# A Mixture-of-Experts, SSM, Mixture-of-Experts block: the middle stage rebuilt, its statistics moved into the expert phase, and TensorE summing the two rotated-back parts

## The reference

```python
x = x + 0.5 * ffn(layernorm(x))     # 8 experts, each token uses the one with the largest logit
x = x + ssm(layernorm(x))           # a diagonal complex recurrence over the 4096 tokens
x = x + 0.5 * ffn(layernorm(x))     # the same weights again

# ffn: logits = x @ Wr; e = argmax; out = softmax(logits)[e] * (gelu(x @ W1[e] + b1[e]) @ W2[e] + b2[e])
# ssm: h_t = a * h_(t-1) + B' @ u_t   (128 complex states);   y_t = real(C @ h_t)
```

## Time and profile before

| | |
|---|---|
| median of 3 runs | 738.88 us (729.33, 738.88, 741.73) |
| the profiled execution | 745.37 us, of which the span from first to last instruction is 743.5 us |
| mean granted PE clock | 0.869 of 2.4 GHz |
| busy share PE, DVE, ACT, POOL | 79%, 71%, 53%, 44% |
| expert phases | 104 to 343 us and 486 to 743 us |
| middle | 343 to 464 us |
| routing | 464 to 486 us |

### The profile page before, as it was taken

How to read it: one execution, slowest core, us unless ns; L and a number is a source line. 1 busy time by engine, 2 the same in 40 slices (tenths; PEclk the granted TensorE clock), 3 DMA queues, 4 the chain that set the end, 5 groups by cost and what they waited for, 6 DMA issues and landing times.

```text
span 743.5 us, 18466 instructions
## 1 busy us (share of the span) xinstructions
PE 589.5 (79%) x6396; PEld 518.0 (70%) x6396; DVE 531.1 (71%) x1204; ACT 396.8 (53%) x879; POOL 330.0 (44%) x310
## 2 busy tenths in 40 slices
PE   5960149999999899994477878139999999999997
PEld 5950138998888787893245657129998778988886
DVE  5869967778886775784499993927776666766675
ACT  4877846565554555552336653107555546546463
POOL 0031183555545453531477881162555454554532
PEclk9555559999999999998658895558999999999999
DMA  8993031111111111113102211030111111111210
GB/s 276 374 375 122 5 99 31 40 45 43 49 45 38 35 51 37 38 30 99 51 29 90 80 57 57 1 103 19 44 51 44 36 50 36 45 41 36 50 36 2
DMA packets 34872, 51.86 MB, mean 70 GB/s; under 512 B 6747, under 2 KB 27933, under 8 KB 34528
## 3 DMA queue, kind: packets, MB, share of 16 engines
q1 hardware_dynamic: 24800, 31.90, 12.6%
q0 software_dynamic: 9984, 18.79, 9.0%
...
...
## 4 chain that ended last, share of the span: by engine, by line
PE 68%; DVE 18%; issue 7%; DMA 3%; ACT 2%; POOL 1%; SPq 1%; ACTq 0%; POOLq 0%; DVEq 0%
PE bank L1065 31%; PE bank L1082 9%; PE bank L1083 9%; PE bank L1084 9%; PE bank L982 4%; PE bank L1041 3%; DVE stats L580 3%; DVE weights_arena L613 2%; PE bank L976 2%; DMA weights_arena<-L_attn_u 2%; DVE weights_arena L920 1%; DVE weights_arena L757 1%; DVE weights_arena L917 1%; DVE weights_arena L942 1%; DVE ev L927 1%
## 5 line engine op out<-in xcount | busy, mean ns | idle before, releaser
L519 ACT ACTIVATE weights_arena<-bank,b1t,inv 128x128 f32<-128x128 f32 x624 | 228.4, 467 | 211.2 <-PE bank L1065 161.2
L1065 PE MATMUL bank<-weights_arena 128*128 128x128 f16 x3744 | 239.2, 222 | 23.5 <-issue 17.5
L1065 PEld LDWEIGHTS bank<-weights_arena 128*128 x3744 | 220.6, 99 | 39.8 <-issue 37.0
L1082 PE MATMUL bank<-weights_arena 128*128 x624 | 170.2, 273 | 1.2 <-issue 1.0
L1083 PE MATMUL bank<-weights_arena 128*128 x624 | 170.1, 273 | 1.3 <-issue 1.1
L1084 PE MATMUL bank<-weights_arena 128*128 x624 | 170.1, 273 | 0.9 <-issue 0.6
L816 DVE TENSOR_SCALAR weights_arena<-weights_arena,hscale 128x512 f16<-128x512 f32 x156 | 76.8, 492 | 83.6 <-ACT weights_arena L519 77.4
L819 DVE SCALAR_TENSOR_TENSOR weights_arena<-weights_arena,hscale 128x512 f16<-128x512 f32 x156 | 117.3, 752 | 5.6
L375 POOL DMA_INDIRECT recf<-records,sorti x78 | 81.4, 1043 | 23.8 <-issue 23.8
L381 POOL DMA_INDIRECT out<-weights_arena,sorti x39 | 39.5, 1013 | 112.7 <-DVE weights_arena L835 99.8
L381 POOL DMA_INDIRECT x_after_ffn<-weights_arena,sorti x39 | 40.6, 1040 | 105.3 <-DVE weights_arena L835 95.8
...
## 6 DMA issues: line engine op xcount, KB each, us to landing
...
recf<-records,sorti POOLq DMA_INDIRECT x78
weights_arena<-L_attn_u,sorti POOLq DMA_INDIRECT x39
x_after_ffn<-weights_arena,sorti POOLq DMA_INDIRECT x39
```

Of the source, the lines that this page charges most:

```text
L519: last = act.activation(hb[q % 2][:, f, :], src, ACT.Gelu, bias=b1t[:, bass.ds(e * FC + f, 1)], scale=inv1[:, bass.ds(e, 1)])
L1065: last = pe.matmul(acc[:, f * P:(f + 1) * P], weights[wpart * DC + d], xts[q % 2][:, xpart, d, :], start=(n == 0), stop=(n == 5))
L1082: pe.matmul(acc, hs[q % 2][:, 0, f, :], high, start=(f == 0), stop=False)
```

## The change

- In the first expert phase DVE takes mean and variance of each finished tile, and POOL its inverse root, deviation and shift. They travel with the rows, in four more columns (rows of 260 numbers instead of 256). The middle loop no longer has `row_stats` for its input.
- The router's logits for the second feed-forward are made by linearity: PE multiplies the transposed normalised input of the recurrence by the centred Wr (`route_logits` right after the B product), DVE scales it back by the deviation (`lt`), and the y product has nine more columns (C times centred Wr, and the row mean), so that DVE only adds. The second normalising, transposing and logit product of the finished rows is gone. ACT takes the variance by squaring finished rows with a running sum, and one inverse root over all tokens follows on POOL after the loop.
- POOL no longer adds the two rotated-back parts: the y product takes both parts, one after the other, into the same PSUM columns (two products for each 128 tokens instead of one). POOL's list now has the sine product of chunk c+1 ahead of the two rotations back of chunk c.
- `zz` has three buffers, `mod` and `uts` two. The state's turn is two small DVE instructions instead of four.
- In both routings one `tensor_scalar` over 1280 numbers becomes a `tensor_tensor`, and 32 small `tensor_scalar` become 4 `tensor_tensor`.

```diff
-LATE = 4
 XS = 5
+XW = D + 4
+MEAN, RSTD, STD, SHIFT = range(D, XW)
+YW = D + E + 1
...
+        zz = [view(11856 + k * 2 * CH, 2, CH) for k in range(3)]
+        waste = view(14928, 3, D, dt=BF16)
+        angle = view(12288, 2, CH)
...
+        psum = ctx.enter_context(nc.psum_tensor("banks", [P, 8, 512], F32))
+        bank = [psum[:, k, :] for k in range(8)]
+        ys = psum[:, 4:8, :]
...
                     pool.wait_ge(s["o"], q + 1)
+                    o = og[q % 2] if ph == 1 else og[q % 2][:, 0:D]
+                    if ph == 1:
+                        ve = ve1[:, q % 2:q % 2 + 1]
+                        pool.wait_ge(o_ve, q + 1)
+                        chain.link(pool.tensor_tensor(o[:, RSTD:RSTD + 1], ve, mhalf[:, 0:1], ALU.pow))
+                        pool.tensor_tensor(o[:, STD:STD + 1], ve, o[:, RSTD:RSTD + 1], ALU.mult)
+                        chain.link(pool.tensor_scalar(o[:, SHIFT:SHIFT + 1], o[:, MEAN:MEAN + 1], -1.0,
+                                                      o[:, RSTD:RSTD + 1], ALU.mult, ALU.mult))
                     pool.indirect_dma_start(dst, bass.IndirectOffsetOnAxis(ap=sorti[:, q, 2:3].bitcast(U32), axis=0),
-                                            og[q % 2], None, bounds_check=T - 1, oob_is_err=False) \
+                                            o, None, bounds_check=T - 1, oob_is_err=False) \
                         .then_inc(s["scat"][q % RING], 16)
...
-            for c in range(-2, NC + 1):
...
+            def rotated(n):
+                pool.wait_ge(s_gs, n + 1)
+                if n >= 2:
+                    pool.wait_ge(s_zi, n - 1)
+                pool.tensor_tensor(mod[n % 2][:, 1, :], gs, turn[:, 1, :], ALU.mult).then_inc(s_mi, 1)
+            rotated(0)
+            for c in range(NC):
+                z = zz[c % 3]
+                if c + 1 < NC:
+                    rotated(c + 1)
+                pool.wait_ge(s_sp, c + 1)
+                pool.tensor_tensor(z[:, 0, :], z[:, 0, :], back[:, 0, :], ALU.mult).then_inc(s_b0, 1)
+                pool.tensor_tensor(z[:, 1, :], z[:, 1, :], back[:, 1, :], ALU.mult).then_inc(s_aa, 1)
+            pool.wait_ge(s_sq, NJ)
+            chain.link(pool.tensor_scalar(ve2[:], ssq[:], 1.0 / D, EPS, ALU.mult, ALU.add))
+            chain.link(pool.tensor_tensor(rstd, ve2[:], mhalf[:], ALU.pow))
+            pool.tensor_tensor(shift, nm2[:], rstd, ALU.mult).then_inc(s_rstd, 1)
             ffn(2, x2_dram, out)
...
             for c in range(-2, NC + 2):
-                if 0 <= c + 1 < NC:
-                    act.wait_ge(s_ut, c + 2)
-                    if c >= 0:
-                        act.wait_ge(s_g, c + 1)
+                n = c + 1
+                if 0 <= n < NC:
+                    act.wait_ge(s_ut, n + 1)
+                    if n >= 2:
+                        act.wait_ge(s_a, n - 1)
                     for d in range(DC):
-                        last = act.copy(uts[:, d, :], bank[d][:])
+                        last = act.copy(uts[n % 2][:, d, :], bank[d])
                     last.then_inc(s_uts, 1)
-                if c >= 2:
...
+                n = c + 2
+                if n < NC:
+                    act.wait_ge(sx[n % XS], 16 * (n // XS) + 16)
                     if n >= 2:
                         act.wait_ge(s_ut, n - 1)
-                    normalise(xs[n % XS], uns[n % 2], lambda i: nb[:, n % 2, i:i + 1],
-                              lambda i: rs[:, n % 2, i:i + 1], s_nb, n + 1, s_un)
+                    x = xs[n % XS]
+                    for i in range(CT):
+                        last = act.activation(uns[n % 2][:, i, :], x[:, i, 0:D], ACT.Identity, bias=x[:, i, SHIFT:SHIFT + 1],
+                                              scale=x[:, i, RSTD:RSTD + 1])
+                    last.then_inc(s_un, 1)
+                n = c + 1
+                if 0 <= n < NC:
+                    act.wait_ge(s_g, n + 1)
+                    if n >= 1:
+                        act.wait_ge(s_mi, n)
+                        act.wait_ge(s_in, n)
+                    act.copy(gs, bank[2]).then_inc(s_gs, 1)
+                b = c - 2
+                if 0 <= b < NC:
+                    act.wait_ge(s_x2, b + 1)
+                    act.wait_ge(s_m2, b + 1)
+                    for i in range(CT):
+                        j = b * CT + i
+                        if j >= 3:
+                            act.wait_ge(s_sq, j - 2)
+                        act.activation(waste[:, j % 3, :], xs[b % XS][:, i, 0:D], ACT.Square, bias=nm2[:, j:j + 1],
+                                       accum_out=ssq[:, j:j + 1]).then_inc(s_sq, 1)
...
-                dve.tensor_scalar(sval[:, :, 1, :], q1, part[:], None, ALU.mult).then_inc(s["pos"], 1)
+                dve.tensor_tensor(sval[:, :, 1, :], q1, part_b[:].unsqueeze(2).to_broadcast([P, NJ, NTE]), ALU.mult).then_inc(s["pos"], 1)
             def route_rows(ph, g):
-                for j in range(GR * g, GR * g + GR):
-                    last = dve.tensor_scalar(onerow[:, j, :], iota_b[:], slot_f[:, j:j + 1], None, ALU.is_equal)
-                last.then_inc(S[ph]["row"], 1)
+                slot_b = placed[ph][10]
+                rows = slice(GR * g, GR * g + GR)
+                dve.tensor_tensor(onerow[:, rows, :], iota_b[:].unsqueeze(1).to_broadcast([P, GR, P]),
+                                  slot_b[:, rows].unsqueeze(2).to_broadcast([P, GR, P]),
+                                  ALU.is_equal).then_inc(S[ph]["row"], 1)
...
+                        dve.wait_ge(s["o"], q + 1)
+                        dve.bn_stats(st1[:], o[:, 0:D]).then_inc(o_stat, 1)
+                        dve.wait_ge(o_stat, q + 1)
+                        dve.bn_aggr(o[:, MEAN:MEAN + 2], st1[:]).then_inc(o_mean, 1)
+                        dve.wait_ge(o_mean, q + 1)
+                        dve.tensor_scalar(ve1[:, q % 2:q % 2 + 1], o[:, MEAN + 1:MEAN + 2], EPS, None, ALU.add) \
+                            .then_inc(o_ve, 1)
...
-            for c in range(-2, NC + LATE):
...
+            for c in range(NC + 1):
+                if c < NC:
+                    m, z = mod[c % 2], zz[c % 3]
                     dve.wait_ge(s_gs, c + 1)
-
-                    dve.tensor_tensor(mod[:, 0, :], gs, turn[:, 0, :], ALU.mult).then_inc(s_in, 1)
+                    dve.tensor_tensor(m[:, 0, :], gs, turn[:, 0, :], ALU.mult).then_inc(s_in, 1)
                     dve.wait_ge(s_in, c + 1)
-                    if c >= 1:
-                        dve.wait_ge(s_aa, c)
-                    dve.tensor_tensor_scan(zz[:, 0, :], rho[:].to_broadcast([P, CH]), mod[:, 0, :], state[:, 0:1],
+                    if c >= 3:
+                        dve.wait_ge(s_y, c - 2)
+                    dve.tensor_tensor_scan(z[:, 0, :], rho[:].to_broadcast([P, CH]), m[:, 0, :], state[:, 0:1],
                                            ALU.mult, ALU.add).then_inc(s_zr, 1)
+                    dve.wait_ge(s_a, c + 1)
+                    dve.tensor_tensor(lt[:, c % 2], bank[3][:, 0:CT * E].rearrange("p (i e) -> p i e", e=E),
+                                      xs[c % XS][:, :, STD:STD + 1].to_broadcast([P, CT, E]), ALU.mult).then_inc(s_lt, 1)
                     dve.wait_ge(s_mi, c + 1)
-                    dve.tensor_tensor_scan(zz[:, 1, :], rho[:].to_broadcast([P, CH]), mod[:, 1, :],
-                                           state[:, 1:2], ALU.mult, ALU.add).then_inc(s_zi, 1)
+                    dve.tensor_tensor_scan(z[:, 1, :], rho[:].to_broadcast([P, CH]), m[:, 1, :], state[:, 1:2],
+                                           ALU.mult, ALU.add).then_inc(s_zi, 1)
                     dve.wait_ge(s_zr, c + 1)
                     dve.wait_ge(s_zi, c + 1)
-
...
+                    zr, zi = z[:, 0, CH - 1:CH], z[:, 1, CH - 1:CH]
+                    link(dve.tensor_scalar(spin[:], rot[:, 1, :], zi, None, ALU.mult))
+                    dve.scalar_tensor_tensor(state[:], rot[:, 0, :], zr, spin[:], ALU.mult, ALU.add).then_inc(s_sp, 1)
+                    dve.wait_ge(s_sp, c + 1)
+                if c >= 1:
                     b = c - 1
+                    x, tokens = xs[b % XS], slice(b * CT, (b + 1) * CT)
+                    dve.wait_ge(s_lt, b + 1)
                     dve.wait_ge(s_y, b + 1)
-                    for h in range(2):
...
+                    dve.tensor_tensor(logits[:, tokens, :], lt[:, b % 2], ys[:, :, D:D + E], ALU.add)
+                    dve.scalar_tensor_tensor(nm2[:, tokens].unsqueeze(2), ys[:, :, D + E:YW], -1.0, x[:, :, MEAN:MEAN + 1],
+                                             ALU.mult, ALU.subtract).then_inc(s_m2, 1)
+                    dve.tensor_tensor(x[:, :, 0:D], x[:, :, 0:D], ys[:, :, 0:D], ALU.add).then_inc(s_x2, 1)
+            dve.wait_ge(s_m2, NC)
...
+                    for d in range(DC):
+                        last = pe.matmul(bank[7][:, 0:E + 1], craw[:, d, :], wr9[:, d, :], start=(d == 0),
+                                         stop=(d == DC - 1))
```

(26 more changed lines are left out.)

235 lines of the change are left out of this document (78 added, 157 removed).

## The result

| | before | changed |
|---|---|---|
| median of the runs | 740.31 us (4 runs) | 767.87 us (4 runs, 766.00 to 774.77) |
| ratio | | 1.048, 95% interval 1.031 to 1.064 |
| profiled execution: time, span | 745.4, 743.5 | 774.8, 772.9 |
| first expert phase, first to last product | 104.0 to 342.4 | 106.3 to 353.7 |
| first rows loaded for the middle | 350.80 | 365.40 |

The change made the kernel slower, by 4.8% as the ratio has it; 3.4% were forecast (764 us). A kernel's executions fall into a faster and a slower state, and every ratio here takes the faster ones alone, so it can differ from that of the medians, which is 1.037. Of the 29.4 us between the two profiled spans, 26.6 are there when the routing begins.

A forecast was written before the change was run, and what follows sets the result against it. The prediction took PE to bound the expert phases and a DVE chain the middle; the new ring's +24.1 us at the routing plus 1.1 in the second routing, on 738.9, gave 764 us, range 735 to 782.

The forecast's parts named there:

- the ring: Middle loop: `gs`, sine product, two rotations back, y product, B product, next `gs`; 16.1 us a chunk against 10.95.
- the alternation: Middle loop: DVE and POOL instructions take turns, 7.0 us from `gs` to the y product; DVE scans 2.4 instead of 1.3.
- Rivals 2 and 3: Middle loop: POOL's products run in a row, 728 or about 747, chance 0.10; DVE and POOL unhindered, 723 or less, 0.12.
- rival 1: Middle loop: the clock stays up through PE's gap; 13.4 us a chunk, 745 us in all, chance 0.17.
- signs of being wrong: y product not waiting for POOL, PE idle below 2 us a chunk, or first expert phase growing over a few us.
- First expert phase, costed at 0: New DVE statistics (0.8 us a tile) and POOL work (at most 1.5) fit into free time: cost 0.
- its end, costed at 2.2: End of the first expert phase: nothing hides the last statistics, 0.8 + 1.4 = 2.2 us later load.
- The upper bound: First expert phase: if half of the new work came through, 0.3 us a tile, 12 us.
- The cold y product: Middle loop: after about 4.8 us without work PE starts at the lower clock, so the y product takes 6.5 us.
- Front, -3.5, then 6.9 to `gs` 1: Start of the middle: statistics and root go, 3.54 us; B product 2.0 and transpose 1.0, `gs` of chunk 1 at 370.3.
- Routings: Entry +0.7 us; second routing +1.1, its root over 32 numbers taking 7.5 us and adding at most 1.
- The old product of the routings: Each routing: the old 2.72 us was a wait behind POOL; the new instruction may wait too, 3.8, a loss of 1.1.

The follow-up runs named there:

- kernel 2: Changed kernel with eight float32 products that nobody reads, made by PE in the gap before each y product but the last two: 756.73 us, ratio 1.026.
- kernel 1: Changed kernel with POOL doing the rotations back of chunk c before the sine product of chunk c+1: 728.56 us, ratio 0.985.
- Kernels 3 and 4: Changed kernel without the first expert phase's statistics on DVE and POOL, 751.13 us; without only POOL's three instructions a tile, 759.47 us.
- kernel 7: kernel 1 with the epsilon added by POOL ahead of its power instead of by DVE: 707.82 us, ratio 1.000.
- experiment 8: kernel 1 with the routings' product of positions again a `tensor_scalar`: 690.98 us, ratio 0.984; once more 724.74 us, ratio 0.978.

## Why the prediction was right, and what was mis-sized

Its mechanism held in every step that the trace can show: the ring of POOL L413, L421, L422, PE L1137, L1145 and ACT's copy; the alternation; PE idle for 4.25 us (4.8 forecast) and then cold (kernel 2 prices it); the order of POOL's list as the place (kernel 1). Rivals 2 and 3 are out by the chain and DVE's rows above, and rival 1 by kernel 2: the clock did not survive the gap, and filling the gap brings 3.81. But the total of +26.6 at the routing, beside a forecast of +24.1, comes from errors that nearly cancel, so how near it came is luck; and one of the prediction's own signs of being wrong came true, the first expert phase grew by more than a few us. By steps:

- **First expert phase, costed at 0: +9.0 us**, and its end, costed at 2.2: 3.3. With the start's 2.3 (0.7 forecast, and within what the start varies by on its own) the first rows came 14.6 us later than before, 2.9 forecast. This step failed. It set 39 x 0.8 = 31 us of new work against 66 free ones. The new work was 41.5 us, since the pause for the expert's number grew with it; and of the 66 us such pauses already took 19.5, in which DVE did nothing else. 41.5 of 46.5 leaves hardly any slack for a list in fixed order that waits for PE and is waited for by it. POOL's share was 1.90 us a tile and not at most 1.5, the 0.83 ahead of the scatter included. The upper bound that the text itself gave, 12 us, was the better estimate. Kernels 3 and 4 give DVE 6.3 and POOL 2.2 of the 9, and kernel 7 shows POOL, with less than 1 us left in a tile, as the second bound.
- **Ring, 16.1 us: 14.45.** `gs` to the y product 6.15, not 7.0: the prediction took the scan at 1.2 and POOL's products at 1.27 each, where each of the five steps behind the cosine product adds only 1.08 (405.49 - 400.08, over five). The cold y product, forecast at 6.5, took 5.85 on average (5.3 to 6.9); idle before it 4.25. That the gap was too long for the clock was taken from a single cold start, behind 3.05; it held in every one of these chunks, but kernel 1 has a gap of 3.11 with the clock up, so it was less sure than it looked. Over six chunks that is -9.9 us, at the end of the stage another -2.3.
- **Front, -3.5, then 6.9 to `gs` 1:** the front took 3.1 us longer than forecast (19.7 us from the first rows to `gs` 1, against 16.6). PE ran at the lower clock there, after 13.56 us without work: the B product of chunk 1 took 3.78 us and its transposes 1.95, which had been put at 2.0 and 1.0. The trace of before had shown it at the same place: the first B product, at 359.59, took 3.78 there too.
- Sum at the routing: 488.0 + 11.7 (start, phase, its end) + 3.1 - 9.9 - 2.3 = 490.6; it began at 490.54.
- **Routings:** the entry's loss fell on L607 and POOL L353, not on the new instruction. The second routing took 22.3 us, 0.6 more than before (1.1 forecast); the power over 32 numbers took 5.50, not 7.5, and was hidden. The second expert phase, with the same code, took 1.8 us longer in this execution; nothing in the change accounts for that (see the last section for how much this phase varies).
- **The old product of the routings.** The prediction read the 2.72 us as a wait behind POOL, which the rows of experiment 8 make likely; it was wrong in the order: the new instruction went ahead of POOL's, and the one after it paid.

The Trainium skill (SBUF — State Buffer, Who interferes with whom) says that a DVE instruction with two SBUF inputs contends with a GpSimd instruction that reads SBUF, and that the shared ports are held by one of them at a time. The trace agrees where both meet, at the entry (3.63 and 4.41) and in the ring (2.14 to 2.18 for instructions that take 1.27 and 1.29 alone).
